# Five routing batches instead of four, earlier scatters, and the second attention's weight products moved behind the first attention's second pass

## The reference

```
x = x + L0_xattn(layernorm(x), ctx, ctx)      # 16 heads of 8, a temperature for each head from statistics of a first softmax
x = x + L0_ffn(layernorm(x))                  # 8 experts, top 2 of each token, hidden 256 (SiLU gate)
x = x + L1_xattn(layernorm(x), ctx, ctx)      # 8 heads of 128, windowed with dilations
x = x + L1_ffn(layernorm(x))                  # 8 experts, top 2, hidden 64 (GELU)
```

## Time and profile before

| | us |
|---|---|
| median of 3 runs | 415.34 (414.65 to 415.39) |
| profiled execution, device time | 413.28 |
| its span | 411.5 |
| PE busy | 353.8 (86%) |
| DVE busy | 303.3 (74%) |
| ACT busy | 271.8 (66%) |
| POOL busy | 196.9 (48%) |
| mean granted TensorE clock | 0.925 of full |

### The profile page before, as it was taken

The page is one execution under the profiler, slowest core; times in us unless marked ns, Lnnn a source line. Parts: engine busy times, 40 slices in busy tenths (PEclk is TensorE's granted clock), DMA queues, the critical chain, the costliest instruction groups (busy, mean ns, idle before and its releaser), DMA issues.

```text
span 411.5 us, 11910 instructions
## 1 busy us (share of the span) xinstructions
PE 353.8 (86%) x4049; PEld 269.5 (65%) x4049; DVE 303.3 (74%) x1127; ACT 271.8 (66%) x813; POOL 196.9 (48%) x295
## 2 busy tenths in 40 slices
PE   2988897682599999973999999888999999968997
PEld 0524362341276767752999998757888888756886
DVE  5399989988428999996764444378898888885852
ACT  2499998986265657542578886457878778672440
POOL 4785878811002215667783000478878783532200
PEclk9988789986589999995799999989999999996999
DMA  7975739700000000112343332111001010000011
GB/s 234 338 212 160 223 100 335 322 1 0 3 2 6 6 5 18 37 34 70 105 116 92 97 92 57 37 33 41 27 23 28 17 28 2 2 2 2 4 49 51
DMA packets 36202, 30.97 MB, mean 75 GB/s; under 512 B 3504, under 2 KB 33584, under 8 KB 35504
## 3 DMA queue, kind: packets, MB, share of 16 engines
q1 hardware_dynamic: 33520, 24.98, 19.2%
q0 software_dynamic: 2048, 4.20, 3.5%
q10 hardware_dynamic: 576, 1.05, 0.7%
HBM read 14.94 MB, written 15.14 MB: 73 GB/s over the span
## 4 chain that ended last, share of the span: by engine, by line
PE 56%; DVE 19%; ACT 9%; issue 8%; POOL 4%; DMA 4%; POOLq 0%; DVEq 0%; SPq 0%; ACTq 0%
PE psum L1753 9%; ACT wa L649 6%; PE psum L1705 5%; PE psum L1545 4%; PE psum L1781 4%; PE psum L1764 4%; DVE scored L1089 3%; DVE scored L1076 3%; PE psum L1585 3%; PE psum L1894 3%; PE psum L1804 2%; PE psum L1688 2%; PE psum L1857 2%; DVE work L1131 2%; PE psum L1820 2%
## 5 line engine op out<-in xcount | busy, mean ns | idle before, releaser
L649 ACT ACTIVATE wa<-psum,scored 128x120 f32<-128x120 f32 x256 | 69.5, 436 | 3.8 <-DVE scored L1076 3.8
L983 POOL DMA_INDIRECT c_area<-by_expert,rows_at x32 | 31.4, 980 | 51.3 <-DMA by_expert<-c_area 39.7
L1089 DVE BATCH_NORM_STATS2 scored<-wa 128x6 f32<-128x240 f32 x128 | 43.1, 398 | 1.6 <-issue 0.8
L1076 DVE TENSOR_REDUCE scored<-psum 128x8 f32<-128x960 f32 x32 | 36.5, 1142 | 9.9 <-PE psum L1585 9.9
L682 ACT ACTIVATE work<-psum 120x1024 f32<-120x1024 f32 x32 | 31.0, 1021 | 18.8 <-PE psum L1693 18.8
L1753 PE MATMUL psum<-c_area,work 128*128 128x128 f32 x312 | 43.3, 284 | 0.0
L1585 PE MATMUL psum<-wa,qT 64*128 64x480 f32 x128 | 41.0, 725 | 2.3 <-ACT wa L649 2.3
L1753 PEld LDWEIGHTS psum<-c_area,work 128*128 128x128 f32 x312 | 39.7, 200 | 0.1
L910 POOL TENSOR_TENSOR rstd<-rstd,eps 128x2 f32<-128x2 f32 x16 | 12.5, 784 | 55.0 <-DVE rstd L1165 55.0
L866 POOL TENSOR_TENSOR wa<-kT,first 128x960 f32<-128x960 f32 x16 | 28.6, 1791 | 16.6 <-PE psum L1585 16.6
L942 POOL DMA_INDIRECT by_expert<-scored,rows_at x32 | 32.2, 1006 | 8.9 <-issue 8.3
(11 more groups left out here) (264 smaller groups left out, 945.0 us busy)
## 6 DMA issues: line engine op xcount, KB each, us to landing
by_expert<-work SPq DMA_DIRECT2D x12, 768.0 KB, 7.6
c_area<-by_expert SPq DMA_DIRECT2D x39, 64.0 KB, 1.8
by_expert<-c_area SPq DMA_DIRECT2D x39, 64.0 KB, 1.6
upT<-in_up_dram SPq DMA_DIRECT2D x1, 2048.0 KB, 13.7
work<-in_heads_dram SPq DMA_DIRECT2D x1, 1536.0 KB, 8.9
late<-in_late_dram SPq DMA_DIRECT2D x1, 1098.0 KB, 10.3
x<-in_x_dram ACTq DMA_DIRECT2D x4, 256.0 KB, 5.6
ctxS<-in_ctx_classes_dram SPq DMA_DIRECT2D x1, 1024.0 KB, 10.0
```

The lines of the kernel that those rows point to most:

```text
L649: e = nc.scalar.activation(prob[:, z, head, :], psum[:, score_bank(b, half) + h // 4, (h % 4) * LK:(h % 4 + 1) * LK], ACT.Exp, bias=rowneg ...
L983: nc.gpsimd.indirect_dma_start(y_rows[:, r, j, :], None, by_expert[:, :], bass.IndirectOffsetOnAxis(rows_at[:, i:i + 1], 0)).then_inc(ld_y ...
L1076: nc.vector.tensor_reduce(rowneg[:, b * H0:(b + 1) * H0].rearrange("p (a c h) -> p a c h", a=2, c=2)[:, :, half], banks(score_bank(b, half ...
L1089: s = nc.vector.bn_stats(bnout[:, bass.ds(b * HALF0 + h // 2, 1), :].rearrange("p a s -> p (a s)"), prob[:, z, h:h + 2, :].rearrange("p h ...
```

## The change

Three things are changed.

1. **Batches** of 4, 3, 3, 3 and 3 sequences (`BATCH_SEQS`) instead of four of 4. There are four phases, of 7, 6, 6 and 20 tiles, still 39 together. Batch 1 is picked at step 12 (before: 13), then one each at 15, 18 and 21 (before 17 and 21). The first table is built in steps 13 to 16. The three other tables are built among the tiles by `TABLES_AT`: two pieces at tile step 0, two at 1, one at each of 2 to 12.
2. **Scatters** by `SCATTERS_AT`: 20 in steps 11 to 18, two or three a step, and 12 behind the loop. Before: two a step in 11 to 18 and 16 behind them, since the steps after 18 have nothing else for POOL.
3. **Products**: groups 0 and 1 at step 18 of pass B, behind the projection of sequence 15, groups 2 and 3 in front of the turn of tiles 4 and 6. Their PSUM banks are 2, 3, 3 and 3. Tile 0's turn, which writes bank 2, now waits for the copy of group 0. The copies of groups 2 and 3 stand in `ct_result` of tiles 3 and 5, behind the wait for that tile's down product.

```diff
-BATCH = 4
-BATCHES, SLOTS = NB // BATCH, 2 * BATCH
+BATCH_SEQS = (4, 3, 3, 3, 3)
+BATCHES = len(BATCH_SEQS)
+BATCH_AT = tuple(sum(BATCH_SEQS[:r]) for r in range(BATCHES + 1))
+MOST_SLOTS = 2 * max(BATCH_SEQS)
+
+def batch_of(b):
+    return next(r for r in range(BATCHES) if b < BATCH_AT[r + 1])
+
+def slots_of(r):
+    return slice(2 * BATCH_AT[r], 2 * BATCH_AT[r + 1])
...
-        seqs = BATCH * (batch + 1)
+        seqs = BATCH_AT[batch + 1]
...
-        PRODUCTS_AT = {0: (0, 1), 1: (2, 3)}
+        PRODUCTS_AT = {NB + 2: (0, 1)}
+        PRODUCT_BANKS = (2, 3, 3, 3)
+        PRODUCTS_CT = {4: 2, 6: 3}
...
-        PIECES_AT = {15: ((0, 0),), 16: ((0, 1), (0, 2)), 17: ((0, 3),), 18: ((0, 4),)}
...
+        PIECES_AT = {13: ((0, 0),), 14: ((0, 1), (0, 2)), 15: ((0, 3),), 16: ((0, 4),)}
+        SCATTERS_AT = ((11, 2), (12, 3), (13, 2), (14, 3), (15, 2), (16, 2), (17, 3), (18, 3))
...
+        TABLES_AT = {0: ((1, 0), (1, 1)), 1: ((1, 2), (1, 3)), 2: ((1, 4),), **{3 + i: ((2, i),) for i in range(5)},
+                     **{8 + i: ((3, i),) for i in range(5)}}
...
             def ct_result(n):
                 act.wait_ge(ct_dn, n + 1)
+                if n + 1 in PRODUCTS_CT:
+                    product_copy(PRODUCTS_CT[n + 1])
...
-            def b_products(b, z):
-                for g in PRODUCTS_AT.get(b, ()):
-                    if g >= 2:
-                        pe.wait_ge(wt_act, g - 1)
+            def b_products(step):
+                for g in PRODUCTS_AT.get(step, ()):
+                    if g == 0:
+                        pe.wait_ge(b_exp, 2 * NB)
                     products(g)
...
             def ct_turn(n):
                 pe.wait_ge(ld_ct[n % RING_C], 16 * (n // RING_C + 1))
+                if n in PRODUCTS_CT:
+                    pe.wait_ge(wt_act, PRODUCTS_CT[n])
+                    products(PRODUCTS_CT[n])
                 if n:
                     pe.wait_ge(ct_xe, n)
+                else:
+                    pe.wait_ge(wt_act, 1)
```

More of the change, by code:

```diff
@@ L84, in slot_of, with seq_at @@
 def slot_of(j, b):
-    r, i = divmod(b, BATCH)
-    return SLOTS * r + BATCH * j + i
+    r = batch_of(b)
+    return 2 * BATCH_AT[r] + BATCH_SEQS[r] * j + b - BATCH_AT[r]
+def seq_at(i):
+    r = batch_of(i // 2)
+    return BATCH_AT[r] + (i - 2 * BATCH_AT[r]) % BATCH_SEQS[r]
 def residue(c):
@@ L524, in load_tile @@
                         for r in range(p.batch + 1) if k == 0 else (p.batch,):
-                            sp.wait_ge(scattered[r], 16 * SLOTS)
+                            sp.wait_ge(scattered[r], 16 * 2 * BATCH_SEQS[r])
                 if n >= RING_C:
@@ L575, in build @@
         RAMP, EARLY_PAIRS = 2, 2
-        PICK_AT = {BATCH * (r + 1) - 1 + LOGITS_B: r for r in range(BATCHES)}
-        TABLE_PIECES = 5
+        PICK_AT = {BATCH_AT[r + 1] - 1 + LOGITS_B: r for r in range(BATCHES)}
         CT_AT = NB + 4
         CT_EARLY = 3
-        PIECES_AT = {15: ((0, 0),), 16: ((0, 1), (0, 2)), 17: ((0, 3),), 18: ((0, 4),)}
-        SCATTERS = {BATCH + LOGITS_B + 1 + i: range(2 * i, 2 * i + 2) for i in range((BATCHES - 1) * BATCH)}
+        PIECES_AT = {13: ((0, 0),), 14: ((0, 1), (0, 2)), 15: ((0, 3),), 16: ((0, 4),)}
+        SCATTERS_AT = ((11, 2), (12, 3), (13, 2), (14, 3), (15, 2), (16, 2), (17, 3), (18, 3))
+        SCATTERS, LOOPED = {}, 0
+        for step, count in SCATTERS_AT:
+            SCATTERS[step] = range(LOOPED, LOOPED + count)
+            LOOPED += count
+        TABLES_AT = {0: ((1, 0), (1, 1)), 1: ((1, 2), (1, 3)), 2: ((1, 4),), **{3 + i: ((2, i),) for i in range(5)},
+                     **{8 + i: ((3, i),) for i in range(5)}}
         def after(first, stage):
@@ L659, in product_copy @@
                 act.wait_ge(wt_ps, g + 1)
-                nc.scalar.copy(product(g)[0], psum[:, 6 + g % 2, :].rearrange("p (i d) -> p i d", d=D)).then_inc(wt_act, 1)
+                nc.scalar.copy(product(g)[0], psum[:, PRODUCT_BANKS[g], :].rearrange("p (i d) -> p i d", d=D)).then_inc(wt_act, 1)
             act.wait_ge(a_dots, NB)
@@ L937, in scatter @@
             def scatter(i):
-                r = i // SLOTS
-                if i % SLOTS == 0:
+                r = batch_of(i // 2)
+                if i == 2 * BATCH_AT[r]:
                     pool.wait_ge(k_rows, r + 1)
@@ L949, in _ @@
             software_pipeline(pool, [(3, tail_rstd("b")), (7, b_scatter)], peel=NB)
-            for i in range(SLOTS * (BATCHES - 1), SLOTS * BATCHES):
+            for i in range(LOOPED, 2 * NB):
                 scatter(i)
@@ L1231, in place_rows @@
                 k_after()
-                row = small[:, 0, SLOTS * NE:SLOTS * (NE + 1)]
+                row = small[:, 0, n * NE:n * (NE + 1)]
                 k_done(nc.vector.tensor_reduce(row, own, AX_X, ALU.add))
@@ L1319, in ct_route @@
             def ct_route(n):
-                if n in range(2 * TABLE_PIECES):
-                    tile_table(1 + n // TABLE_PIECES, n % TABLE_PIECES)
-                elif n == TILES - 4:
+                for piece in TABLES_AT.get(n, ()):
+                    tile_table(*piece)
+                if n == TILES - 4:
                     expert_weights()
@@ L1615, in products, with b_products @@
                 for i in range(4):
-                    m = nc.tensor.matmul(psum[:, 6 + g % 2, i * D:(i + 1) * D], left[:, i], right[:, i], start=True, stop=True)
+                    m = nc.tensor.matmul(psum[:, PRODUCT_BANKS[g], i * D:(i + 1) * D], left[:, i], right[:, i], start=True, stop=True)
                 m.then_inc(wt_ps, 1)
-            def b_products(b, z):
-                for g in PRODUCTS_AT.get(b, ()):
-                    if g >= 2:
-                        pe.wait_ge(wt_act, g - 1)
+            def b_products(step):
+                for g in PRODUCTS_AT.get(step, ()):
+                    if g == 0:
+                        pe.wait_ge(b_exp, 2 * NB)
                     products(g)
@@ L1721, in rank @@
                     pe.wait_ge(k_rows, r)
[L1722 removed]
+                cells = rank_ps[:, 0:n * NE].rearrange("p (i e) -> p i e", e=NE)
                 nc.tensor.matmul(cells, tri_b[:, :], picked[:, at], start=True, stop=False)
                 if r:
[L1725 removed]
+                    nc.tensor.matmul(cells, ones_b[:, :], seen[:, r - 1, :].unsqueeze(1).to_broadcast([P, n, NE]),
                                      start=False, stop=False)
[L1727 removed]
+                for i in range(n - 1):
                     nc.tensor.matmul(cells[:, i + 1:], ones_b[:, :],
[L1729 to L1730 removed]
+                                     picked[:, at.start + i, :].unsqueeze(1).to_broadcast([P, n - 1 - i, NE]), start=False, stop=False)
+                m = nc.tensor.matmul(rank_ps[:, 0:n * NE], ones_b[0:1, :], region_b[:, 0:n * NE], start=False, stop=True)
                 if r in [p.batch for p in PHASES]:
```

34 lines of the change are left out of this document (17 added, 17 removed).

## The result

The changed kernel takes 417.01 us (median of 20 executions) against 414.99 for the kernel before beside it, also 20: ratio 1.0072, interval [1.005, 1.0094]. The change makes the kernel slower, as forecast; the forecast was +2.35 us, this measurement says +2.0 by the medians.

A forecast was written before the change was run, and what follows sets the result against it. PE and DVE were taken as full in pass B, POOL's waits as limiting the drain, PE as the bound among the tiles. Eight terms sum to +2.35 us on the 415.34 median: 417.7, range 414.3 to 419.5.

The forecast's parts named there:

- Term 1: Start of pass B: products leave, freeing 3.1 us, most of it given back by a later clock rise; -0.9 us.
- Terms 2 to 4: Drain: step 17 starts 3.0 later, three scatters delay norm 15 by 2.8, first-load wait goes; +0.1 us.
- POOL isn't late: Drain rival: steps 12 to 16 stretch otherwise than thought, -2.2 us, total 415.5, no change; chance 0.08.
- the 2 in 10 outside: Whole kernel: chance left for times outside the range 414.3 to 419.5 us.
- Term 5: First tiles: DVE also makes second-table pieces 3 and 4 between evictions of tiles 0 and 3; +0.55 us.
- Terms 6 and 7: Among the tiles: two product groups cost PE their full time, +2.0 us; PE waits for ACT's group 2 copy, +0.7.
- Term 8: Among the tiles: a table-piece delay leaves tile step 4 (-0.5), a new one comes at step 7 (+0.4); -0.1 us.
- the clock is also held in the drain: Drain rival: moved products hold 2.4 GHz into the first up products, about 1.2 us saved; 414.3 with front -3.1; chance 0.16.
- move as a block: Behind the tiles: the second attention and everything after it shift together.
- the three signs that would have made the forecast wrong: Front, drain, tiles: clock rising before 117, powers of 14 and 15 under 4 us apart, PE not waiting for the copy.

The follow-up runs named there:

- e6: Changed kernel plus five products that nobody uses behind the scores of sequence 0; 415.19 us, ratio 1.0017.
- e1: Kernel before with only the products placed as in the change, old batches and scatters kept; 414.83 us, ratio 1.0002.
- e3: Changed kernel with no scatter at step 17 and six at step 18, behind the power of sequence 15; 415.19 us, ratio 1.0008.
- e4: Changed kernel with ACT's copies of product groups 2 and 3 one tile step sooner; 416.72 us, ratio 1.0063.
- e5: Kernel before with product groups 0 and 1 left at the front, groups 2 and 3 moved into the drain; 412.97 us, ratio 0.996.
- e11: Repetition of the kernel before with groups 0 and 1 at the front, 2 and 3 in the drain; 410.96 us, ratio 0.9869.
- e9: Changed kernel unaltered, measured a third time against the kernel before; 416.93 us, ratio 1.0011.
- e0: Changed kernel unaltered, measured a second time against the kernel before; 415.80 us, ratio 1.0034.

## Why the prediction held, point by point

Numbers are us against the kernel before, from the first scores of pass B.

| term | forecast | measured |
|---|---|---|
| 1 front | -0.9 | -0.86 |
| 2 to 4 drain, up to tile 0's eviction, without the front | +0.1 | +0.03 |
| 5 DVE's queue in the first tiles | +0.55 | +0.4 |
| 6 products among the tiles | +2.0 | +2.0 |
| 7 wait for the copy | +0.7 | +0.77 |
| 8 table hiccups | -0.1 | +0.4 |
| clock rises sooner in the first tiles | not in the sum | -1.0 |
| sum at the keys | +2.35 | +1.8 (the rows above add up to 1.7) |

- **Term 1** is right in size and cause. The rise came at 119.8 where I had worked out 118.5 to 119.8 and wrote near 119, the reciprocal at 120.70 where I said near 120.2 (in an execution whose pass A was 0.40 later). e6 shows the cause. The delay that I carried over, 5.0 us, is 5.2 by the earlier trace rows, and in the profiles with the gap it is 4.0 to 6.2 from the second scores on; that it fitted within 0.4 here is partly luck, since e1 has a gain of 0.2.
- **Terms 2 to 4.** Step 17 came 2.5 later, 3.3 with the front's gain taken out; I said 3.0. The powers stand 4.50 apart (4.7), the DVE waits 1.63 for the last (about 2), the norm comes 2.8 later (2.8). e3 shows that it is POOL. (The prediction's rival "POOL isn't late" is priced at 2.2 but asks for an error of only 1.5; these don't go together. And the chances it names add up to 1.00, which leaves nothing for the 2 in 10 outside.)
- **Term 5**: of the 0.55, the first rank product's wait for the DVE and the fuller queue took 0.4 up to tile 3. I worked this out as up 0 to up 3, 7.30 against 6.91, less 1.0 for the product block, plus 1.0 for the clock.
- **Terms 6 and 7** are in PE's rows; e4 takes the wait away. Up of tile 5 comes 12.1 behind up of tile 0, not the 13.1 that I wrote: the 1.0 is the clock, below.
- **Term 8 is mis-sized.** I priced the new hiccup at step 7 like the old ones, 0.4. Up of tile 8 comes 2.28 behind that of tile 7, where a steady tile takes 1.45: 0.83. The last table's is 0.45 (before 0.39), and the 0.51 at tile 5 is gone: together +0.4. The last piece of the third table runs on the DVE in front of the eviction that PE waits for, from its first row to its last 1.27 us in all:

```profile
210.17 0.23 DVE L1307 TENSOR_SCALAR tile_tab<-scratch 1x6 uint32<-1x6 f32 x1
...
211.44 0.35 DVE L1357 TENSOR_SCALAR c_area<-psum,first 128x128 f32<-128x128 f32 x1
```

- **What the sum lacked** is the clock in the first tiles. The rival "the clock is also held in the drain" was half right. The clock did fall in the changed kernel's drain, but it rose sooner, in the middle of tile 1's up product. In this order two stretches of the changed kernel:

```profile
196.00:198.00 2.00, 1.82 (x16) 1.44 (x15) 1.83 (x7) 0.89 (x2) 1.70 (x2) 0.50 0.31 98
198.00:200.00 2.00, 1.98 (x16) 1.82 (x16) 1.77 (x11) 0.83 (x3) 1.39 (x3) 0.92 0.28 82
```

  Before, 198 to 200 ran at 0.50 and the rise came at about 200.7, by the 0.83 of the earlier trace rows; the prediction's 200.4 is a misreading. So tile 1's up product takes 1.35 (1.38 and 1.25 in the two repetitions) instead of 1.92 and the down product behind it 0.61 instead of 1.06: 1.0 us. PE had more to do here: in the changed kernel it is busy 1.26 of 2 us at 192 to 194, before 0.02. That this is the cause is not shown: e6, with the same program here and PE busy 1.24 and 1.38 of 2 us at 192 to 196, has 1.92.
- **Behind the tiles** the block didn't quite move as a block. From the keys to the end it takes 154.0 instead of 154.55. The clock differs there too: 268 to 272 in the changed kernel, then in the kernel before:

```profile
268.00:272.00 4.00, 1.89 (x24) 1.09 (x21) 2.38 (x12) 1.36 (x2) 3.02 (x6) 1.00 0.07 17
```

```profile
268.00:272.00 4.00, 3.45 (x29) 1.64 (x32) 2.04 (x9) 1.36 (x2) 3.20 (x5) 0.62 0.13 33
```

  In e5 this place ran at 0.50 and in its repetition e11 at 1.00, so it is a chance of the execution and not the change's doing. With +1.8 at the keys, -0.6 behind them and +0.4 before pass B the span is 1.6 longer.

None of the three signs that would have made the forecast wrong appeared. But the total came out near the forecast partly by luck: the mis-sized hiccup (+0.5) and the missed clock (-1.0) partly cancel, and of the four figures for the total (+2.0 and +3.0 here, +0.5 and +1.4 by the medians of the repetitions) two lie well below 2.35. The structure, that PE among the tiles pays in full and that the drain's wait changes its owner, is what the runs confirm.

## What to carry to other kernels

- Work that leaves a place takes the engine's cover with it: before the product blocks are moved, look at whether they fill a gap before the clock has risen, and at which engine's queue the freed wait falls next. The three scatters in front of the last power on POOL cost 1.5 to 2.0 us at tile 0 (e3): work that nobody waits for belongs behind the instruction that another engine needs.
- Filler belongs where the engine waits anyway (the drain, some 0.15 us for 2 us of products), not where it is the bound (the tiles, 1.0 us each and a wait for the copy besides). With a shared PSUM bank, count the reader's place in its own engine's queue, not only its duration.

## What the runs showed that I had not expected

- **More work, an earlier end of the stage.** Five useless products (2.50 us at low clock) on the engine that is the bound brought the first reciprocal 1.4 to 1.6 us sooner (e6).
- **The clock can dip while PE is mostly busy, and where it does differs between executions of one kernel.** The changed kernel in its first profile, with PE busy 1.27 of 2 us in the stretch before and 2.00 of 2 in the one shown:

```profile
182.00:184.00 2.00, 2.00 (x46) 1.85 (x40) 1.83 (x13) 0.25 (x2) 1.59 (x2) 0.50 0.13 41
```

  Its third profile, e9, has the same 0.50 there. Its second, e0, held 1.00 until 192. The dip stretched the output of sequence 15 to 1.94 and 1.73 us from 1.08 and 1.06. So gains at the marks below some 0.5 us, the scatter of the changed kernel's own three executions, can't be read from one profile each.
- **Pass A's length** moves by 4 us between executions of identical code (first scores of pass B at 108.8 to 112.9). For a change of 0.5%, marks that count from the start of the stage that was changed told more than the total did.
